# A filter product read straight from its PSUM bank, and a fourth bank for the second filter product

## The reference

```python
# second layer; ssp(x) = softplus(x) - ln 2
bf  = exp(coeff * (dist[:, None] - centers[None, :]) ** 2)
bf  = ssp(bf @ W1 + b1)
bf  = ssp(bf @ W2 + b2)
cut = where(dist < 5, 0.5 * (cos(pi * dist / 5) + 1), 0)
msg = h[src] * edge_feat * bf * cut[:, None]
agg = segment_prod(msg, dst)
out = ssp(agg @ W3 + b3)
```

## Time and profile before

| | |
|---|---|
| median of 3 runs | 4655.83 us (4644.31 to 4661.99) |
| profiled execution | 4661.2 us, its span 4659.4 us |
| busy over the span | PE 3628.6 us (78%), DVE 3161.9 (68%), ACT 2724.9 (58%), POOL 1914.3 (41%) |
| product stage | about 2572 to 4554 us |
| instructions | 67064 |

### The profile page before, as it was taken

How to read it: one execution, slowest core, us unless ns; L and a number is a source line. 1 busy time by engine, 2 the same in 40 slices (tenths; PEclk the granted TensorE clock), 3 DMA queues, 4 the chain that set the end, 5 groups by cost and what they waited for, 6 DMA issues and landing times. The chain is left out here.

```text
span 4659.4 us, 67064 instructions
## 1 busy us (share of the span) xinstructions
PE 3628.6 (78%) x23091; PEld 2344.5 (50%) x23091; DVE 3161.9 (68%) x5677; ACT 2724.9 (58%) x4265; POOL 1914.3 (41%) x1883
## 2 busy tenths in 40 slices
PE   5888889899999999999998566666666666666663
PEld 4777777444554455444544344444444444444442
DVE  9999999423333233332312788888888888888886
ACT  3666665322222222222200899999999989999983
POOL 6222000401000000100011677777777777777774
PEclk9888888999999999999999778788777778878775
DMA  4333333778887888887875666666666666666762
GB/s 139 131 134 131 124 129 129 239 242 250 247 248 225 245 246 245 249 247 243 248 229 167 193 198 194 199 195 202 197 195 200 199 195 199 195 198 194 201 186 76
DMA packets 641678, 920.75 MB, mean 198 GB/s; under 512 B 69714, under 2 KB 423239, under 8 KB 641431
## 3 DMA queue, kind: packets, MB, share of 16 engines
q1 hardware_dynamic: 550727, 782.85, 52.2%
q0 software_dynamic: 59936, 119.71, 10.9%
q10 hardware_dynamic: 30768, 15.26, 1.2%
HBM read 674.96 MB, written 242.59 MB: 197 GB/s over the span
## 5 line engine op out<-in xcount | busy, mean ns | idle before, releaser
L1311 POOL DMA_INDIRECT hgat<-x_rows,edge_src x1564 | 1504.6, 962 | 490.1 <-issue 475.1
L953 PE MATMUL bank<-gran,hp 128*128 128x490 bf16 x7056 | 1504.1, 372 | 28.6 <-DVE hp L1098 28.6
L953 PEld LDWEIGHTS bank<-gran,hp 128*128 128x128 bf16 x7056 | 677.3, 96 | 822.7 <-DVE hp L1098 30.1
L815 POOL DMA_INDIRECT x_sb<-h_rows,last_i x147 | 138.7, 943 | 1503.6 <-DMA h_rows<-h_out 1469.1
L1388 PE MATMUL bank<-c_b,one_b 96*128 96x512 bf16 x309 | 140.2, 454 | 744.4 <-DVE efl L1454 677.1
L1439 DVE TENSOR_SCALAR bank<-rows_e,edge_same,edge_first 128x128 f32<-128x128 f32 x1564 | 645.1, 412 | 42.5
L611 PEld LDWEIGHTS bank<-hi_hot,lo_hot 128*128 128x128 bf16 x7840 | 546.0, 155 | 217.8 <-issue 69.6
L611 PE MATMUL bank<-hi_hot,lo_hot 128*128 128x49 bf16 x7840 | 574.1, 219 | 94.7 <-DVE hi_hot L403 93.4
L527 ACT CAST stage<-bank 128x490 bf16<-128x490 f32 x784 | 451.9, 577 | 308.1 <-PE bank L611 297.4
L1019 DVE TENSOR_SCALAR t<-bank,c_sb 128x512 f32<-128x512 f32 x82 | 61.6, 751 | 826.3 <-PE bank L928 816.6
L1388 PEld LDWEIGHTS bank<-c_b,one_b 96*128 96x128 bf16 x309 | 30.5, 99 | 1019.9 <-issue 984.1
(11 more groups left out here) (237 smaller groups left out, 4485.9 us busy)
## 6 DMA issues: line engine op xcount, KB each, us to landing
gran<-step_counts SPq DMA_DIRECT2D x336, 857.5 KB, 4.9
dist<-weight_by_step SPq DMA_DIRECT2D x391, 256.0 KB, 4.6
running_products<-rows_e SPq DMA_DIRECT2D x391, 256.0 KB, 3.7
step_counts<-stage SPq DMA_DIRECT2D x112, 857.5 KB
ef<-in_edge_attr SPq DMA_DIRECT2D x391, 224.0 KB, 4.2
hgat<-x_rows,edge_src POOLq DMA_INDIRECT x1564
kn<-keep_and_norm_of_steps SPq DMA_DIRECT2D x48, 490.0 KB, 6.8
edge_filter_times_attr<-g_out SPq DMA_DIRECT2D x82, 256.0 KB, 3.5
```

Of the source, the lines that this page charges most:

```text
L953: last = nc.tensor.matmul(y, hp[:, 7 * g + i, part, :], gran[:, g, :, i * IS:(i + 1) * IS], start=first, stop=last_)
L1311: pool.indirect_dma_start(out=hgat[:, b % U, c, :], out_offset=None, in_=x1_d, in_offset=bass.IndirectOffsetOnAxis(ap=edge_src[:, b, c:c + ...
```

## The change

The filter of a block in `MADE_IN_D` stays in its PSUM bank. `finish` multiplies by the edge features in place, and `products` reads the filter from the bank instead of from `efl`. The bank is therefore free only after that block's product, and `z2(f)` waits for `s_v` instead of `s_fin`. `ps2` gets bank 7 as a fourth bank, so that this wait is for filter f - 4. The wait of `finish` for a free slot of `efl` is gone. The blocks of `MADE_IN_C` are as before.

```diff
-            ps1, ps2 = banks[0:R], banks[R:2 * R]
+            Z = R + 1
+            ps1, ps2 = banks[0:R], (*banks[R:2 * R], banks[7])
...
-                            nc.scalar.activation(l, ps2[f % R][:], ACT.Relu, bias=soft_max[:], scale=-1.0
+                            nc.scalar.activation(l, ps2[f % Z][:], ACT.Relu, bias=soft_max[:], scale=-1.0
...
-                            if f >= R:
-                                pe.wait_ge(s_fin, f - R + 1)
-                            z = ps2[f % R]
+                            if f >= Z:
+                                pe.wait_ge(s_v, block_of(f - Z) + 1)
+                            z = ps2[f % Z]
...
                                 dve.wait_ge(s_fin, MADE_IN_D[b] + 1)
+                                filters = ps2[MADE_IN_D[b] % Z][:].rearrange("p (c d) -> p c d", d=D)
                             else:
                                 dve.wait_ge(s_fi[b % U], loads_of(b))
+                                filters = efl[:, b % U]
...
-                            nc.vector.tensor_tensor(prod_e[:, b % R], hgat[:, b % U], efl[:, b % U], ALU.mult
+                            nc.vector.tensor_tensor(prod_e[:, b % R], hgat[:, b % U], filters, ALU.mult
...
-                            b = block_of(f)
                             dve.wait_ge(s_l24, f + 1)
-                            g = ps2[f % R][:]
+                            g = ps2[f % Z][:]
...
-                            dve.wait_ge(s_v, b - U + 1)
-                            nc.vector.tensor_tensor(efl[:, b % U].rearrange("p c d -> p (c d)"), g, ef4[:, f % Q],
-                                                    ALU.mult).then_inc(s_fin, 1)
+                            nc.vector.tensor_tensor(g, g, ef4[:, f % Q], ALU.mult).then_inc(s_fin, 1)
```

## The result

The changed kernel takes 4640.35 us (median of 10 runs, 4635.45 to 4642.97); the kernel before takes 4654.16 (10 runs). The ratio is 0.9966 with a 95% interval of 0.9958 to 0.9974: a gain of 15.8 us, between 12 and 20 (the two medians differ by 13.8). The profiled execution took 4641.5 us, span 4639.7, against 4661.2 and 4659.4.

A forecast was written before the change was run, and what follows sets the result against it. POOL's 1564 gathers were taken to bound the product stage. Only term 1 counted: median 4655.8 - 20.2 = 4635.6, say 4636 us; the forecast's own range was 4627 to 4645, the stated range 4626 to 4657.

The forecast's parts named there:

- Term 1: Block product of the 309 made blocks: filter read from PSUM, so it holds no gather; 20.2 us off POOL's path.
- Term 2: Products of the 82 loaded blocks still read two SBUF tiles and keep 8.3 us of stretch, range 0 to 15.
- rival B: Stretch at the 82 loaded blocks goes as well, as the phase moves off gather starts: 28.2 us, 4628; chance 0.10.
- Term 3: Filter's last step writes its PSUM bank in place: 689 ns against 692, 309 x 3 ns, about nothing.
- rival C: In-place PSUM write costs up to 0.484 us per filter, DVE becomes the wall: 13 us longer, 4669; chance 0.04.
- Term 4: Fourth bank for the second filter product: PE's and ACT's waits shrink or move behind POOL; costed at nothing.
- what would show it: Signs of being right: mean gather near 949 ns, stretch only beside loaded blocks, PE's wait for DVE well below 677 us.
- The tail: End of the product stage, after the last gather: shifts as a whole, within a microsecond.
- A: Gathers stay held beside the block product, or for another cause; only hidden waits move: 4656; chance 0.15.
- D: Extra bank is worth more because ACT or PE is the true limit; no time of its own worth a chance.

The follow-up runs named there:

- the two runs that split the change: Kernel before with a fourth bank for the second filter product, filter still in efl: 4655.3 us; changed kernel with three banks instead of four: 4639.1 us.
- the kernel with the copies: Changed kernel with three banks; ACT copies 76 of 82 loaded filters from efl to bank 7, where the product reads them: 4630.2 us, ratio 0.9941.

## Why the prediction was right, point by point

The forecast was 4636 us, a gain of 20.2; measured are 4640.35 and a gain of 15.8 (12 to 20). The time, and that it lies within 0.5% of before, are as forecast. The stated range, 4626 to 4657, took in "no change" as well, so that the time lies in it says little; what bears out the mechanism are the traces and the experiments. The base moved too: with more runs the median of the kernel before is 4654.2 instead of 4655.8.

- **POOL is the wall.** Shown: the idle time before a gather is 0.305 us in both kernels, and 5% fewer gathers took 84 us off.
- **Term 1, the product of the made blocks.** Shown: 20.2 us of stretch before, none after in three profiles, and none with the operands exchanged, the form that no row had. The fourth bank alone, with the product left SBUF-fed, brought nothing. The mean of three profiles is 19.6.
- **Term 2, the loaded blocks.** The mechanism was right and its size off. I kept 8.3 us with 0 to 15 as range; in the profile after it is 11.6, in the mean of three 10.6 against 8.3. This is the larger part of what the sum missed, 2.3 of the 4.4 us between 20.2 and 15.8. Executions of one kernel differ by as much (8.5 to 11.7). My reason against rival B, that products which wait for rows fall worse against a regular POOL, is not what happened. Loaded products that had waited for their rows have 6.5, 6.8 and 6.8 us of stretch in the three profiles before and 6.5, 4.0 and 5.6 in the three after. Those that had not waited went from 1.8, 0.9 and 1.9 us to 5.1, 4.5 and 6.1. The rise is theirs, and that B failed was not for the reason I gave; why they meet more gathers stays open.
- **Term 3, the write in place.** 700 ns against 692, where I said 689: 309 x 8 ns = 2.5 us on DVE, hidden. The dearer write of rival C, 0.484 us each, is excluded.
- **Term 4, the fourth bank.** Nothing, as costed. PE's wait did not fall "well below 677 us", though, as I wrote under what would show it; it was 724. A wait that is not on the path need not shrink when its cause is eased.
- **The tail.** I allowed a microsecond; the three profiles give 107.9 against 106.8 us, 1.1 longer. It need not come with the change: with the operands exchanged the tail is 105.7 us, with three banks 106.7.

Together: -19.6 + 2.3 + 1.1 = -16.2 us by six profiles, against -15.8 (12 to 20) measured. The part of the sum that was off in size is term 2.

Of the rivals, A (the hold stays) is excluded by the traces. So is, for these gathers, the inference in the Trainium skill's page SBUF — State Buffer, "Who interferes with whom", that a tensor_tensor does not hold descriptor generation: 191 of the 238 gathers that start inside the product of the kernel before are stretched. Whether the making of descriptors is held or something the gather reads first, no run separates. The same section's rule that an instruction with at most one SBUF input, outside the modes that use two ports, does not contend agrees with the 208 gathers inside PSUM-fed products. C is excluded by term 3, and D by the two runs that split the change. B came out the other way in this kernel, and was reached only by an edit made for it.

## What to carry to other kernels

Where GpSimd's indirect DMAs set the pace, look at their longest durations, not at their mean alone, and match their starts with what DVE runs then; a tensor_tensor of DVE with two SBUF inputs lengthened them here, and moving one input to PSUM freed them at next to no cost to DVE (687 ns instead of 692 for the product, 700 instead of 692 for the multiply ahead of it). Two SBUF inputs are not the only such case: a tensor_scalar from SBUF to SBUF held gathers too, as told below. The bank for it may come out of a pipeline that does not need it, and an engine with idle time, here ACT, can pay for a copy. Waits of 700 us on PE were worth nothing here, while of 28 us hidden inside instructions that counted as busy, the kernel with the copies got back 25 to 28.

## What the runs showed of the hardware that I had not expected

How long a gather is held follows one line: the gather of 3635.10 started with 0.58 us of the product left and took 0.45 us longer, that is the rest of the product less about 0.13 us. Over the stretched gathers beside SBUF-fed products of that profile, what is taken off lies between 0.12 and 0.13 us. A gather that had started before the product was not held, nor one that started in its first 0.04 us. There the product gave way: it ended 0.72 us behind the start of the gather, as here, and took up to 0.76 us instead of 0.69.

```profile
3887.09 0.76 DVE L1427 TENSOR_TENSOR prod_e<-hgat,efl 128x512 f32<-128x512 f32 x1 [0.34 <-DMA hgat<-x_rows,edge_src]
3887.12 0.94 POOL L1312 DMA_INDIRECT hgat<-x_rows,edge_src  x1 [0.30 <-issue]
```

So whichever of the two comes first holds the other, and a product lost less than 0.08 us by it.

The first gather of the stage takes 0.18 to 0.19 us more than 0.944 in every profile, and no product runs then. In the changed kernel it starts 0.04 us into a cast of DVE from SBUF to SBUF, which has one tensor input:

```profile
2568.84 0.36 DVE L1460 CAST c_hi<-c_all 96x512 bf16<-96x512 f32 x1
2568.88 1.13 POOL L1312 DMA_INDIRECT hgat<-x_rows,edge_src  x1 [13.53 <-issue]
```

The rest of the cast, 0.32 us, less 0.14 is the 0.18 found. It is also a first gather after a long idle time, but the one of line 1317, after 11.56 us of idle time, took 0.94. With one such gather in a run, this is a reading and not shown.

A tensor_scalar with one SBUF tile as input and an SBUF tile as output held gathers too (101 of 207 starts inside it, 3.2 us; those in its first 0.15 us were not held), and ran in 369 ns in the mean instead of 412; with its output in PSUM neither is seen. The Trainium skill, SBUF — State Buffer, "Who interferes with whom", has the first: a tensor_scalar may enter a mode with two ports and then contend. That this short f32 form did so is my reading of the two numbers. The 369 ns hide two cases: the median is 346 ns, and 220 of the 1564 took 450 ns or more. These 220 had started 0.40 us or more behind the start of a gather, and each ended about 0.05 us behind the end of that gather:

```profile
3126.71 0.94 POOL L1312 DMA_INDIRECT hgat<-x_rows,edge_src  x1 [0.31 <-issue]
3127.13 0.57 DVE L1442 TENSOR_SCALAR factors_sb<-rows_e,edge_same,edge_first 128x128 f32<-128x128 f32 x1
```

No SBUF-fed product waited in this way; the longest took 0.77 us.

In one execution POOL was slower as a whole. One-line view of the gathers of the stages before, in the first and in the second run of the kernel with the copies:

```profile
L815 POOL DMA_INDIRECT x_sb<-h_rows,last_i x147: 942/947/994, 1014.0 to 2556.9; - x147
```

```profile
L815 POOL DMA_INDIRECT x_sb<-h_rows,last_i x147: 938/944/977, 1011.6 to 2555.5; - x147
```

The median is 947 ns against 944 there, and in the product stage as well (941/947/1133 against 940/944/1202), 0.3% in all; over 1564 gathers that is 5 us, and that execution took 4635.7 us against 4630.6. The expectation that it belonged to the execution and not to the kernel held.
